# Three input DMAs on ScalarE's queue instead of SyncE's, in a four-layer conditional residual kernel

## The reference

```python
x = x + L0(x, cond_8)   # w_bot[b] = sum_g cond[b, g] * (weight[g] * mask); x @ w_bot.T + bias
x = x + L1(x, cond_8)   # expert argmax(cond[b]); (silu(x Wu + bu) * (x Wg + bg)) Wd + bd, hidden size 512
x = x + L2(x, cond_8)   # the two best experts, weighted, and a shared one: (gelu(x G) * (x U)) D, hidden size 1024
x = x + L3(x, cond_8)   # x W_base.T + b_base + 2 * sum_e cond[b, e] * (x A_e.T) B_e.T
```

## Time and profile before

| what | value |
|---|---|
| median of 3 runs | 509.38 us (508.44 to 509.86) |
| the profiled execution | 509.63 us |
| its span, first to last instruction | 507.8 us |
| TensorE busy | 497.8 us, 98% of the span |
| VectorE, ScalarE busy | 343.7 us (68%), 259.1 us (51%) |
| mean granted TensorE clock | 0.997 |
| moved by DMA | 51.65 MB |

### The profile page before, as it was taken

The page is one execution under the profiler, slowest core; times in us unless marked ns, Lnnn a source line. Parts: engine busy times, 40 slices in busy tenths (PEclk is TensorE's granted clock), DMA queues, the critical chain, the costliest instruction groups (busy, mean ns, idle before and its releaser), DMA issues.

```text
span 507.8 us, 6580 instructions
## 1 busy us (share of the span) xinstructions
PE 497.8 (98%) x2159; PEld 404.9 (80%) x2159; DVE 343.7 (68%) x606; ACT 259.1 (51%) x402; POOL 0.2 (0%) x4
## 2 busy tenths in 40 slices
PE   8897999999999999999999999999999999999996
PEld 3675888888888888888888888888888888888885
DVE  6695687776766678676677756575675666655645
ACT  3654555455654454456665535355654555444541
POOL 0000000000000000000000000000000000000000
PEclk9998999999999999999999999999999999999999
DMA  8942133333232242233233333222333233231002
GB/s 269 398 138 59 68 93 98 101 105 102 94 94 94 94 124 83 84 95 95 91 115 103 95 104 97 90 94 93 95 93 100 88 122 96 93 94 32 1 0 83
DMA packets 20625, 51.65 MB, mean 102 GB/s; under 512 B 2928, under 2 KB 3568, under 8 KB 20592
## 3 DMA queue, kind: packets, MB, share of 16 engines
q1 hardware_dynamic: 20592, 51.24, 31.4%
HBM read 49.13 MB, written 2.10 MB: 101 GB/s over the span
## 4 chain that ended last, share of the span: by engine, by line
PE 94%; DVE 2%; DMA 1%; ACT 1%; issue 1%; SPq 0%; DVEq 0%
PE act_ps L259 10%; PE act_ps L261 10%; PE act_ps L260 10%; PE lin_ps L259 10%; PE lin_ps L260 10%; PE lin_ps L261 10%; PE acc_ps L259 10%; PE acc_ps L260 10%; PE acc_ps L261 10%; PE aux_ps L259 1%; PE aux_ps L260 1%; PE aux_ps L261 1%; PE acc_ps L307 1%; DMA w<-w_in 1%; DVE hid L610 1%
## 5 line engine op out<-in xcount | busy, mean ns | idle before, releaser
L608 DVE TENSOR_TENSOR hid<-lin_ps,act 128x512 f32<-128x512 f32 x96 | 66.4, 691 | 109.1 <-PE lin_ps L261 108.9
L599 DVE TENSOR_TENSOR w_lo<-raw,w_hi 128x384 fp32r<-128x384 f32 (+1 forms) x222 | 122.7, 553 | 1.4 <-ACT w_hi L381 1.4
L387 ACT ACTIVATE act<-act_ps 128x512 f32<-128x512 f32 x96 | 57.4, 598 | 124.6 <-PE act_ps L261 124.6
L393 ACT ACTIVATE hid_hi<-hid 128x512 fp32r<-128x512 f32 x112 | 70.8, 632 | 86.8 <-DVE hid L608 73.1
L381 ACT ACTIVATE w_hi<-raw 128x768 fp32r<-128x768 f32 x112 | 93.9, 838 | 0.0
L616 DVE TENSOR_TENSOR hid_lo<-hid,hid_hi 128x512 fp32r<-128x512 f32 x112 | 77.4, 691 | 23.8 <-ACT hid_hi L393 23.8
L259 PE MATMUL act_ps<-x_hi,w_hi 128*128 128x512 f32 x228 | 89.2, 391 | 3.1 <-ACT w L422 2.1
L261 PE MATMUL act_ps<-x_hi,w_lo 128*128 128x512 f32 x228 | 89.0, 390 | 0.0
L260 PE MATMUL act_ps<-x_lo,w_hi 128*128 128x512 f32 x228 | 88.9, 390 | 0.0
L259 PE MATMUL lin_ps<-x_hi,w_hi 128*128 128x512 f32 (+1 forms) x226 | 88.1, 390 | 0.0
L261 PE MATMUL lin_ps<-x_hi,w_lo 128*128 128x512 f32 (+1 forms) x226 | 88.0, 389 | 0.0
(11 more groups left out here) (78 smaller groups left out, 311.9 us busy)
## 6 DMA issues: line engine op xcount, KB each, us to landing
raw<-w_in SPq DMA_DIRECT2D x112, 384.0 KB, 3.0
w<-w_in SPq DMA_DIRECT2D x8, 256.0 KB, 5.6
x<-x_in SPq DMA_DIRECT2D x4, 512.0 KB, 5.7
out<-x SPq DMA_DIRECT2D x7, 256.0 KB, 3.7
mask<-mask_in SPq DMA_DIRECT2D x1, 256.0 KB, 5.8
base<-base_in SPq DMA_DIRECT2D x1, 256.0 KB, 7.8
out<-x SPq DMA_DIRECT2D x2, 128.0 KB, 2.0
lora_b<-lora_b_in SPq DMA_DIRECT2D x1, 128.0 KB, 5.6
```

The source lines that it names most:

```text
L387: act_e.activation(act[:, n % 2, :], act_ps[:, n % 2, :], func, bias=bias).then_inc(act_ready, 1)
L393: act_e.activation(hid_hi[:, n % 2, :], hid[:, n % 2, :], ACT.Copy).then_inc(hid_hi_ready, 1)
L599: ins = dve.tensor_tensor(w_lo[:, n % SPLIT, a:z], raw[:, n % RAW, a:z], w_hi[:, n % SPLIT, a:z].bitcast(F32), ALU.subtract)
L608: ins = dve.tensor_tensor(hid[:, n % 2, :], lin_ps[:, n % 2, :], act[:, n % 2, :], ALU.mult)
```

## The change

SyncE's first issue becomes the layer-0 weights of expert 0. The issues of cols, ident and x of row 0 move to ScalarE's stream, in this order, ahead of its first wait. All transfers keep their source, target, size and semaphore.

```diff
-            sp.dma_start(cols[:, :], cols_d).then_inc(cols_in, 16)
-            sp.dma_start(ident[:, :], ident_d).then_inc(ident_in, 16)
             for g in range(E):
                 sp.dma_start(w0[:, g, :], w0_d[:, g, :]).then_inc(w0_in[g], 16)
-                if g == 1:
-                    sp.dma_start(x_row(x_flat, 0), x_d[0]).then_inc(x_in[0], 16)
                 if g == 5:
                     sp.dma_start(mask[:, :], mask_d).then_inc(mask_in, 16)
             sp.dma_start(lora_b[:, :], lora_b_d).then_inc(lora_b_in, 16)
@@
+            act_e.dma_start(cols[:, :], cols_d).then_inc(cols_in, 16)
+            act_e.dma_start(ident[:, :], ident_d).then_inc(ident_in, 16)
+            act_e.dma_start(x_row(x_flat, 0), x_d[0]).then_inc(x_in[0], 16)
             act_e.wait_ge(zeros_ready, 1)
             act_e.wait_ge(route, 3)
             act_e.activation(r_exp[:, :, :], r_prob[:, :, :], ACT.Exp).then_inc(route_exp, 1)
```

## The result

| | median | runs | lowest to highest |
|---|---|---|---|
| before | 509.3 us | 20 | 507.45 to 510.24 |
| changed | 511.6 us | 20 | 509.03 to 512.31 |

The ratio is 1.004, 95% interval 1.0028 to 1.0053: the change costs 0.3 to 0.5%. The forecast was 508.7 us and no measurable change. The profiled execution of the changed kernel took 511.8 us with a span of 510.0, 2.2 above that of before.

The account below looks back on a forecast made before the run. The prediction took TensorE to bound the kernel, busy for 497.8 of 507.8 us. Earlier expert 2 weights were to save 0.7 us, with no cost from ident, taking the median from 509.38 to 508.7 us, range 508.2 to 509.3.

Parts of the forecast that it names:

- ident decides when VectorE starts: Step on the kernel's head: VectorE's diagonals wait for ident, and a small delay of it was to cost nothing.
- The cover: VectorE's idle 1.63 us before the mask, which hides a later ident; 1.3 us left after the assumed delay.
- d: How much later ident comes at the head than before; taken as 0.3 us, with 0 to 1.8 considered.
- a landing after 5: Sign named beforehand that the prediction is wrong: ident at the head landing after 5 us.
- The upper end: Largest delay of ident considered, 1.8 us, from the 3.8 us a 5 KB transfer takes in a full queue.
- The rule of turns between the rings: DMA engines alternate between rings packet by packet, so ident's 512-byte rows wait for 2 KB weight rows; delay near 0.9 us.
- What I drew from it for expert 2: At the head, expert 2's weights were to land at 7.5 us and not at 7.0.
- ident comes late: Rival at VectorE's diagonals: each microsecond of ident's delay beyond 1.63 us costs the kernel one; chance 0.06.
- a chance that the loss disappears: Rival that the low clock after TensorE's wait shortly before 48 us goes away, giving 507.2 us; chance 0.15.
- A low clock appears: Rival that a new low-clock stretch comes near 5 to 8 or near 38 us, giving 510.4 us; chance 0.05.
- the 0.7 forecast: Gain at the start of the mask from expert 2's earlier weights, 0.7 us, with ends of 0.1 and 1.5.

Follow-up runs that it names:

- e2: The changed kernel with x back behind expert 1 in SyncE's queue, cols and ident still on ScalarE's; median 509.42 us, ratio 1.0016.
- e4: The changed kernel with 12 idle TensorE products on zeros between the layer-0 sum and layer 0; median 510.39 us, ratio 1.0026.
- e6: The changed kernel with copy_lora(3) moved earlier on ScalarE, before the split of tile 6; median 507.21 us, ratio 0.9975.
- e7: The changed kernel with VectorE's sum_w0(1, 3) moved behind the mask and split of row 0; median 509.46 us, ratio 1.0022.
- e10: The changed kernel with copy_lora(3) early, 12 idle products before layer 0 and 12 warmup products instead of 9; median 506.60 us.
- e3: The changed kernel with SyncE waiting until ident has landed before it issues the first weights; median 510.71 us, ratio 1.0029.
- e8: The changed kernel with ident alone back at the head of SyncE's queue, cols and x still on ScalarE's; median 507.83 us, ratio 0.9993.
- e11: The kernel before with copy_lora(3) early and cols alone moved to ScalarE's queue, x behind expert 1 on SyncE's; median 505.31 us, ratio 0.9929.
- e5: The kernel before with copy_lora(3) moved earlier on ScalarE, before the split of tile 6; median 505.64 us, ratio 0.9947.
- e9: The kernel before with copy_lora(3) early, a repeat of e5 as base for e10, e11 and e12; median 505.69 us, ratio 0.9936.
- e12: As e11, but x behind expert 2 instead of expert 1 in SyncE's queue; median 505.61 us, ratio 0.9928.
- e1: The changed kernel with cols and ident back at the head of SyncE's queue, only x on ScalarE's; median 509.83 us, ratio 1.0015.

## Why the prediction was wrong

**The step that failed** is the paragraph "ident decides when VectorE starts", in its last sentences. The cover was named and sized right: 1.63 us, less what ident comes later. The size of d was not. I took 0.3, with a range from 0 to 1.8, because the engines carried little yet when ident flew in the earlier trace rows. But the change itself puts the weights beside it. d was 2.2 us in the profiled execution and 2.1 to 2.7 in e2, e4, e6, e7 and e10 (starts of the diagonals at 5.46 to 6.06 against 3.33), outside the range; e3, which takes the weights away, has 0.0. ident landed at 5.5, and the prediction had named a landing after 5 as a sign that it is wrong. The upper end was the worst of the bounds: a 5 KB transfer behind others in one queue says nothing about one that shares its engines with a second queue at the slow start of the transfers.

The rule of turns between the rings had pointed the right way (the Trainium skill, DMA: Bandwidth & Descriptors, "Queues, rings and completion order"): the trace agrees in the direction, and by 2.2 against my estimate of 0.9 from it not in the size. The estimate also took a row for a packet, where that section counts 9 to 17 descriptors to one. The other rule, that issuing from several engines saves only issue time (the same page of the Trainium skill, "Issuing engines are not separate DMA queues"), agrees with e8 and e11: the diagonals start 0.4 to 0.5 us earlier there than before, one issue, and in e8 x on the second queue takes from expert 0 what it gives to the others. What I drew from it for expert 2 is not borne out: it landed at 6.9, not at 7.5, ahead of x at 7.3. Nothing hung on that.

**The rival "ident comes late"** had the mechanism and the price of the delay: d = 2.2 gives 2.2 - 1.63 = 0.57 us, and the mask came 0.51 later; e10 has 0.9 in the time. Its point of decision was wrong: "slower by over 0.3% needs d above 3.1". It counted only VectorE's delay. It overlooked that TensorE, with its sum done earlier, then waits 2.9 us instead of 1.5, and that the profile of before already had an example of what follows such a wait: 2.1 us of waiting and then a granted clock of 0.50. I had used that example only as a chance that the loss disappears. "A low clock appears" stood beside it as a rival of its own with 0.05 and at other places (near 5 to 8 us and near 38), though the late ident brings it about behind the sum: 12 of 20 runs have two recorded stretches, and none of the 35 runs of before has.

**Right** were: expert 0 issued at 0.74 and landed at 3.9; ScalarE's issues hidden under its wait; x in time (1.67 + 5.6 = 7.3); nothing behind 15 us changed but by the shift and the clock. The first `sum_row0` product was to start at 5.05 and started at 5.97, held by its diagonal; TensorE still ended 0.8 us earlier, close to the 0.7 forecast, but that is in part luck. The forecast let the sum start at 5.05 with slow records and no hole behind expert 1; in fact it started 0.9 late and ran its records 0.43 apart from the second on. The gain lies idle in the wait of 2.9 us. Of SyncE's queue I wrote that the first tile would go out at 9.89 as before; it went at 12.11, since the expert numbers stand behind ident on VectorE, but it cost nothing here.

**Open** is why the low stretch behind a wait comes in some runs and not in others: two stretches are recorded in 2 of 10 runs of e2 with a wait of 2.7 us in its profile, and in 12 of 20 of the changed kernel with 2.9. The profiles show one execution each and no experiment varied the wait alone. Also open is the loss of the five changed runs of clock 1.000: 1.6 us above before, where e10 gives 0.9 to the late ident; a stretch in the sum that isn't recorded, as in e6, may be the rest, but none of the five was profiled. And no run put ident behind a weight transfer in one and the same queue, so it isn't shown how much of d comes from the second queue and how much from weights that are merely issued earlier.

## What to carry to other kernels

A second queue doesn't make the head of a kernel faster when the small transfer on it is what everything waits for: put the few kilobytes that start the chain first, with nothing large issued ahead of them in either queue, and look at how long the smallest transfer is in flight before and after. When an engine finishes earlier than what it waits for next, its wait grows; on TensorE a wait of 2.1 to 2.9 us cost itself and, in about half of the runs here, 1.6 to 1.9 us of low clock behind it, so a delay of 0.5 us became 2.2. And a known wait in the middle of the kernel (here a copy that stood behind two instructions that it didn't need) was worth 2.9 and 3.8 us in the medians of e5 and e9, where the best order of the head (e11) added 0.4, within the spread of the runs.

## What the runs showed of the hardware that was not expected

- A 64 KB transfer (ident) took 1.9 to 2.3 us where no large one had been issued ahead of it (before, e3, e5, e8, e9, e11, e12), 3.3 us with 512 KB issued 0.5 us earlier on the other queue (e1), and 4.2 to 4.8 us with 256 KB issued there 0.4 us earlier and 256 KB more beside it (the changed kernel, e2, e4, e6, e7, e10). Expert 0's 256 KB went from 3.4 to 5.4 us with 512 KB beside it (e8).
- The kernel before has runs at 507.8 and at 509.7 us, 1.9 apart, and the mean granted clock (1.000 or 0.997) tells them apart.
- The column of granted clock reads 1.00 over the first 14 us before and after, and in e3 and e6, while the distance between equal products of the sum changes from about 0.86 to 0.43 us within them (before, e3, e6), and the same 16 records take 7.12, 9.10 or 9.64 us.
